# An attention kernel whose steady heads compute the scores of tile 6 ahead of the transpose of the preceding head's tile 0

## What is computed

```python
q = rmsnorm((xn @ Wq.T).reshape(heads))
k = rmsnorm((xn @ Wk.T).reshape(kv_heads))
v = (xn @ Wv.T).reshape(kv_heads)
rel = pos[None, :] - pos[:, None]
bias = where(rel > 0, -1e30, slope[h] * rel)
attn = softmax(q @ k.T / sqrt(128) + bias)
s = (attn @ v) @ Wo.T
g = silu((silu(xn @ gate) * (xn @ up)) @ down)
out = x + s * g
```

## Time and profile before

| | |
|---|---|
| median of 3 runs | 1289.11 us (1289.05 to 1289.66) |
| the profiled execution | 1288.81 us |
| its span in the profile | 1286.9 us |
| PE busy | 1274.3 us, 99% |
| DVE, ACT, POOL busy | 960.2, 650.3, 703.9 us |
| granted TensorE clock | 0.999 |

### The profile page before, as it was taken

The page is one execution under the profiler, slowest core; times in us unless marked ns, Lnnn a source line. Parts: engine busy times, 40 slices in busy tenths (PEclk is TensorE's granted clock), DMA queues, the critical chain, the costliest instruction groups (busy, mean ns, idle before and its releaser), DMA issues.

```text
span 1286.9 us, 21247 instructions
## 1 busy us (share of the span) xinstructions
PE 1274.3 (99%) x7141; PEld 1098.4 (85%) x7141; DVE 960.2 (75%) x2081; ACT 650.3 (51%) x1441; POOL 703.9 (55%) x758
## 2 busy tenths in 40 slices
PE   8999999999999999999999999999999999999998
PEld 7888888888888888888888888888888888888886
DVE  6555555578778777777787778777877787778887
ACT  4322222265665555555555555555555555555552
POOL 4855555535565455545554555455545554555486
PEclk9999999999999999999999999999999999999999
DMA  7554445120010001000000000000000100000211
GB/s 200 158 143 127 127 129 129 28 82 18 17 34 17 17 18 33 18 17 18 33 18 18 17 34 17 18 17 34 18 17 18 34 17 17 17 18 17 99 58 66
DMA packets 31966, 62.09 MB, mean 48 GB/s; under 512 B 3840, under 2 KB 4096, under 8 KB 31744
## 3 DMA queue, kind: packets, MB, share of 16 engines
q1 hardware_dynamic: 31872, 60.88, 16.2%
HBM read 56.67 MB, written 4.19 MB: 47 GB/s over the span
## 4 chain that ended last, share of the span: by engine, by line
PE 88%; DVE 6%; issue 2%; ACT 2%; POOL 2%; DMA 0%; DVEq 0%; POOLq 0%
PE O L1120 31%; PE O L1185 13%; PE S L1724 12%; PE T L1141 9%; PE S L1164 5%; PE S L1167 5%; PE S L1165 5%; DVE pb L855 2%; POOL pb L437 1%; PE O L1739 1%; PE T L1739 1%; PE O L1740 1%; PE T L1740 1%; PE O L1738 1%; PE T L1738 1%
## 5 line engine op out<-in xcount | busy, mean ns | idle before, releaser
L437 POOL TENSOR_TENSOR pb<-rel,coef 128x1024 f32<-128x1024 f32 (+7 forms) x256 | 292.9, 1159 | 140.6 <-PE T L1141 135.8
L579 ACT ACTIVATE pb<-pb,low 128x1024 f32<-128x1024 f32 (+7 forms) x256 | 198.8, 777 | 188.8 <-DVE low L855 188.5
L839 DVE TENSOR_TENSOR pt_l<-T,pt_h 128x512 fp32r<-128x512 f32 (+3 forms) x384 | 209.9, 550 | 43.8 <-ACT pt_h L569 43.8
L569 ACT ACTIVATE pt_h<-T 128x512 fp32r<-128x512 f32 (+3 forms) x384 | 181.9, 485 | 105.8 <-PE T L1141 104.0
L855 DVE CUSTOM_DVE_ANT_0 pb<-S,pb,ninv 128x1024 f32<-128x1024 f32 (+7 forms) x256 | 207.6, 811 | 34.2 <-PE S L1167 28.7
L1141 PE MATMUL T<-ident,pb 128*128 128x128 f32 x1152 | 183.4, 273 | 5.3 <-DVE pb L864 3.3
L864 DVE TENSOR_SCALAR pb<-pb,rinv 128x1024 f32<-128x1024 f32 (+7 forms) x256 | 167.8, 656 | 9.0
L1141 PEld LDWEIGHTS T<-ident,pb 128*128 128x128 f32 x1152 | 139.7, 140 | 39.5 <-DVE pb L864 6.8
L1164 PE MATMUL S<-kT_h,q_h 128*128 128x512 f32 (+2 forms) x384 | 141.2, 368 | 0.0
L1185 PE MATMUL O<-pt_h,v_h 128*128 128x512 f32 (+2 forms) x384 | 140.9, 367 | 0.1
L397 POOL TENSOR_TENSOR wo_l<-wo_in,wo_h 128x512 fp32r<-128x512 f32 x32 | 41.3, 1292 | 169.0 <-ACT wo_h L622 169.0
(11 more groups left out here) (185 smaller groups left out, 2900.1 us busy)
## 6 DMA issues: line engine op xcount, KB each, us to landing
wq_in<-in_wq SPq DMA_DIRECT2D x32, 256.0 KB, 2.8
wo_in<-in_wo SPq DMA_DIRECT2D x32, 256.0 KB, 2.6
stage<-in_wkv SPq DMA_DIRECT2D x8, 512.0 KB, 3.9
pb<-in_gate_w SPq DMA_DIRECT2D x14, 256.0 KB, 2.6
pb<-in_gate_z SPq DMA_DIRECT2D x14, 256.0 KB, 3.6
pb<-in_gate_s SPq DMA_DIRECT2D x14, 256.0 KB, 4.9
pb<-in_up_w SPq DMA_DIRECT2D x14, 256.0 KB, 5.3
pb<-in_up_z SPq DMA_DIRECT2D x14, 256.0 KB, 6.2
```

What stands on the lines that cost most here:

```text
L437: g_.tensor_tensor(pbuf(idx, t), rel[:, TOK - w:TOK], coef[:, t:t + 1].to_broadcast([P, w]), ALU.mult).then_inc(bias_ready, 1)
L569: a_.activation(pt_lot(pt_h, t, n), bank[:, 0:m * P].rearrange("p (k w) -> p k w", w=P), ACT.Copy).then_inc(tr_hi, 1)
L579: a_.activation(pbuf(idx, t), pbuf(idx, t), ACT.Exp, bias=low[:, idx:idx + 1], scale=-1.0, accum_out=rsum[:, idx:idx + 1]).then_inc(exps_r ...
L839: v_.tensor_tensor(pt_lot(pt_l, t, n), bank[:, 0:m * P].rearrange("p (k w) -> p k w", w=P), f(pt_lot(pt_h, t, n)), ALU.subtract).then_inc( ...
```

## The change

In heads 1 to 3 of each steady group, 18 heads in all, the scores of tile 6 are put in front of T0, as in the other groups. The branch for steady groups goes away.

```diff
                 if prev:
                     lots(h - 1, 1)
-                if j > 0 and kind == "steady":
-                    q_proj(at, f"qc0_{j}", h, {6: [lambda h=h: lots(h - 1, 0), lambda h=h: scores(h, 1)]})
-                elif j > 0:
+                if j > 0:
                     q_proj(at, f"qc0_{j}", h, {6: [lambda h=h: scores(h, 1), lambda h=h: lots(h - 1, 0)]})
```

## The result

The changed kernel takes 1298.74 us (median of 4 runs, 1298.48 to 1298.83) against 1289.17 for the kernel before (4 runs): 9.57 us more, a ratio of 1.0074 with a 95% interval from 1.0062 to 1.0086. It is slower, as forecast, and 0.5 us off the forecast of 1299.2.

What follows compares the result with a forecast made beforehand. PE, busy 99% of the span, was taken as the bound, so added waits lengthen the kernel directly. Waits of 0.55, 0.59 and 0.55 us make 1.69 a group, 10.1 over six: 1289.11 becomes 1299.2 us, range 1297.0 to 1302.6.

Steps and rivals of the forecast that it cites:

- T0 1.22 us later, no wait of PE removed: On PE, T0 (transpose of the preceding head's tile 0) moves from 1.60 to 2.82; neither it nor the scores behind waited.
- The swap itself costs PE nothing: On PE, scores of tile 5 start at 7.51 in head 7 and 7.46 in head 29, 0.05 us apart.
- head 29: Last-group head already in the changed order, taken as the same sequence measured: transposes of tile 5 at 13.62, 0.24 us wait.
- ACT's exponentials 1.23 us later: On ACT, T0's copy stands ahead of tile 7's exponentials, which move from 2.08 to 3.31.
- DVE's reciprocal 1.24 us later, 0.67 absorbed, 0.57 left: On DVE, the reciprocal moves from 3.35 to 4.59; idle times absorb 0.67, so tile 6's low part starts 0.57 us later.
- The transposes of tile 5 0.55 us later, 1.69 us a group, 10.1 in all: PE's transposes wait for DVE's low part of tile 6: 13.62 against 13.07; six groups give 10.1 us.
- A new wait at the scores of tile 5, which start at 7.99 to 8.07, not added to step 5: PE waits about 0.5 us for DVE's sums of squares in steady heads; the sum stays 0.55 a head.
- Everything behind moves as a whole: Behind the waits in PE's in-order queue, the head moves whole; DVE, ACT and POOL move with it.
- The first rival, no effect: Nothing reaches PE because DVE makes up 1.24 us before tile 5's transposes; time 1289.1 or 1288.2 us; chance 0.05.
- The second rival, the doubled lateness: POOL's tile 4 bias holds DVE's next normalising, each steady head losing 0.57 us more: 1309.5 us; chance 0.06.

Runs made afterwards that it cites:

- exp_first_pool_waits: exp_first plus one POOL wait: in steady heads 1 to 3 tile 4's bias starts only after DVE has normalised tile 7; 1287.91 us, repeated 1287.97 us.
- sums_first: Changed kernel, but in steady heads 1 to 3 DVE takes the sums of squares before the low part of Q; 1299.12 us.
- exp_first: Changed kernel, but in steady heads 1 to 3 ACT takes tile 7's exponentials before T0's copy; 1289.92 us.
- four places of T0: T0 starting at 1.60 (kernel before), 2.07 (pair_later), 2.81 (changed kernel) and 3.27 (t0_later_still) of the head: 1288.97, 1288.67, 1298.74 and 1307.04 us.
- t0_later_still: Changed kernel with T0 two matmuls later still in the steady heads' first Q projection, tile 6's scores staying put; 1307.04 us.
- pair_later: Kernel before, with T0 and tile 6's scores, in the old order, two matmuls later in steady heads 1 to 3; 1288.67 us.
- t0_first_all: Kernel before, with T0 ahead of tile 6's scores also in heads 1 to 3 of the first and last group; 1293.31 us.
- norm_first: exp_first, with DVE's normalising of tile 7 also put before T0's low part in steady heads 1 to 3; 1290.22 us.
- combined: All groups' heads 1 to 3: changed PE order, ACT's exponentials first, low part of Q first, POOL's biases behind DVE's normalising; 1287.63 us.

## Why the prediction was right

By its own steps:

1. *T0 1.22 us later, no wait of PE removed.* 1.21 measured.
2. *The swap itself costs PE nothing.* Shown by exp_first_pool_waits, which has the changed order on PE and is not slower than the kernel before. In sums_first the scores of tile 5 start at 7.45, the 0.05 us earlier that head 29 had promised.
3. *ACT's exponentials 1.23 us later.* 1.21. That this queue order is the cause is shown by exp_first.
4. *DVE's reciprocal 1.24 us later, 0.67 absorbed, 0.57 left.* 1.20, 0.68 and 0.52. The four places of T0 give 0.71 for the slack, read at PE instead of on DVE; it rests on the slope of one that t0_later_still shows.
5. *The transposes of tile 5 0.55 us later, 1.69 us a group, 10.1 in all.* 0.50 in head 7, 1.60 a group, 9.6 in all. The term is over-sized by 5%, for the most part since DVE in head 29 came to its reciprocal at 4.59 and in the changed head 7 at 4.55.
6. *A new wait at the scores of tile 5, which start at 7.99 to 8.07, not added to step 5.* The wait is there 18 times; they start at 7.92. sums_first shows that it is not an addend: without it the time is the same.
7. *Everything behind moves as a whole.* The six groups are lengthened by 1.60 each and nothing is given back later.

The first rival, no effect, was wrong in the place it had named: DVE had 0.7 us of slack and needed 1.2. pair_later shows that it would have been right for a shift of 0.47. The Trainium skill (Perfetto Trace Analysis, Identifying the Most-Contended Engine) says to optimise the engine with the highest occupancy first. As a forecast for a change of order it is of no use here: PE's work is the same in all kernels, and the times go from 1287.6 to 1307.0. The second rival, the doubled lateness, did not occur in the changed kernel (0.75 us for the normalising), but it was a live one, since in exp_first the same two instructions meet. Its condition, POOL's bias ending after DVE's reciprocal, and its price, forecast at 0.57 from a neighbouring row, were about right: 0.46 us on the instruction. Most of that was absorbed there, because DVE was only 0.28 us late otherwise.

In one reading the prediction was lucky. It took head 29 for the steady sequence with T0 later, and its wait of 0.24 us for one lost "by order alone". t0_first_all shows otherwise: with T0 first, head 29 has its exponentials at 3.31 all the same and waits at the same transposes. In the kernel before, two things come out together there: T0's copy starts at 1185.76, which lets the exponentials start 0.18 us later, as in head 7 of the changed kernel; the logits' extreme is read at 1185.83, which lets them start 0.11 us later, as in head 29 of t0_first_all (1187.13 to 1187.24). Both give 1185.94. Only so does head 29's 3.31 agree with T0's lateness added to head 7's 2.08, and only so did its 13.62 give the price to 0.05 us. What makes the prediction's path right is not head 29 but the steady heads themselves, in exp_first and the four places of T0. What head 29 did rightly give is DVE's 8.19 us without idle time, from the reciprocal on.

What stays open: why one head of norm_first has an issue gap of 0.24 us on DVE, and how the 0.57 us that head 31 of combined loses at its product with V become 0.92 by the end.

## What to carry to other kernels

When an instruction on a full engine moves, find who copies its result out and what stands behind that copy in the copier's queue; the price is the lateness less the idle time between there and the next place at which the full engine waits, and past that knee it is one for one. A stretch of the same trace that has the changed order already is the best source of that price, but check that its inputs are as early as in the place that is changed; in head 29 they were not, and the price came out right by a coincidence. A wait that the profile names may be only the first place where a late queue is met: here taking it away moved it 5.7 us down the head and won nothing.

## What the runs showed of the hardware that was not expected

- POOL's TENSOR_TENSOR on SBUF tiles and DVE's TENSOR_SCALAR from SBUF to SBUF did not run side by side in these traces; whichever started first ran at its length. Ahead by 0.06 us, DVE kept 0.75 us and POOL took 1.81 instead of 1.25; with POOL ahead by 0.26 us, POOL kept 1.25 and DVE took 1.54, ending 0.55 us after POOL (0.56 in exp_first). The Trainium skill (SBUF — State Buffer, SBUF: two separate sides) calls it an exclusive lock for the whole instruction; the trace agrees. A start that differs by a few tenths of a microsecond in one head of 18 then cost 1.1 us on PE.
- DVE's logits, which read PSUM and one large SBUF tile, were not held: for 1024 keys they take 1.28 us in the changed kernel's head 7, with a POOL bias beside them most of the time, and 1.27 in head 29 of the kernel before, between two biases.
- The idle time in brackets is less than what a wait on PE costs by starting times. In the changed head 7 eight transposes start at 482.05 and the scores at 483.31, 1.26 us later; in sums_first they are 0.79 us apart (481.85 and 482.64). So the wait costs 0.47 us, and the bracket says 0.23. Over 18 heads the waits are listed at 4.1 us of the 9.6, and PE's busy time went from 1274.3 to 1280.3 us with no work added. Positions in the head tell the cost, sums of waits don't.
